# A message-passing network with experts on one core: the experts' input as a pipeline of tile groups

## What is computed

```python
h = jnp.maximum(_layernorm(x, axis=-1), 0.0)
x = x + _L3_gnn_ref(h, edge_index, ...)

def _L3_gnn_ref(x, edge_index, W_in, b_in, router_W, ...):
    h = x @ W_in + b_in                      # 3125 x 256
    for l in range(3):
        agg = segment_sum(h[src], dst) / deg
        logits = concatenate([h, agg]) @ router_W[l] + router_b[l]
        ...
        h = h + conf * moe
    return h @ W_out + b_out
```

## Time and profile before

| | |
|---|---|
| three runs, median | 3355.61 us |
| three runs, lowest and highest | 3353.94 and 3356.59 us |
| the profiled execution, its own time | 3354.32 us |
| its span, first to last instruction | 3352.3 us |
| mean granted clock of PE | 0.961 |
| busy: PE, DVE, ACT | 89%, 65%, 27% of the span |

### The profile page before, as it was taken

One profiled execution on the slowest core, in us unless ns is written; L12 is line 12 of the kernel. 1 busy time (PEld: TensorE's weight loads), 2 busy tenths in 40 slices (PEclk: granted clock), 3 DMA queues, 4 the chain that ended last, 5 costly groups with the idle time before them and its releaser, 6 DMA issues. The chain is left out here.

```text
span 3352.3 us, 47544 instructions
## 1 busy us (share of the span) xinstructions
PE 2990.9 (89%) x18761; PEld 1803.0 (54%) x18761; DVE 2184.1 (65%) x3982; ACT 897.6 (27%) x1667; POOL 16.6 (0%) x22
## 2 busy tenths in 40 slices
PE   3777889999797999999959999988999998999997
PEld 2555555555343444444535655664656564566565
DVE  7999555554426667666666666675666675666666
ACT  3887322121212000000023222323222233222222
POOL 1000000000000000000000000000000000000000
PEclk8898999999898999999979999998999998999999
DMA  4544456563003555554330000002000002000001
GB/s 103 155 140 145 134 184 205 189 209 125 21 1 116 172 154 171 171 155 130 88 104 4 6 3 4 3 3 80 3 4 4 5 1 82 3 4 3 4 3 40
DMA packets 310670, 262.56 MB, mean 78 GB/s; under 512 B 32735, under 2 KB 289377, under 8 KB 308142
## 3 DMA queue, kind: packets, MB, share of 16 engines
q1 hardware_dynamic: 295406, 252.86, 24.7%
q10 hardware_dynamic: 14624, 5.76, 0.7%
q0 software_dynamic: 416, 0.85, 0.1%
HBM read 171.03 MB, written 88.41 MB: 77 GB/s over the span
## 5 line engine op out<-in xcount | busy, mean ns | idle before, releaser
L1437 PE MATMUL psum<-r_wd,r_h 128*128 128x512 fp8e4 (+1 forms) x2600 | 567.9, 374 | 13.3 <-ACT r_h L226 12.7
L2057 PE MATMUL psum<-m_agg,m_weights 128*128 128x512 f16 (+2 forms) x2016 | 423.1, 362 | 34.2 <-ACT m_agg L1964 34.2
L2018 PE MATMUL psum<-counts,m_h 128*128 128x512 fp8e4 (+2 forms) x2100 | 416.0, 354 | 29.0 <-DVE m_h L1754 29.0
L2076 PE MATMUL psum<-m_weights,x_nodes 128*128 128x256 f16 (+1 forms) x3600 | 413.0, 273 | 17.6 <-DVE m_wtmp L1862 15.9
L1437 PEld LDWEIGHTS psum<-r_wd,r_h 128*128 128x128 f16 x2600 | 240.0, 96 | 306.1 <-issue 16.8
L2076 PEld LDWEIGHTS psum<-m_weights,x_nodes 128*128 128x128 f16 (+1 forms) x3600 | 350.3, 98 | 75.1 <-DVE m_wtmp L1862 22.6
L2057 PEld LDWEIGHTS psum<-m_agg,m_weights 128*128 128x128 f16 x2016 | 197.3, 101 | 243.1 <-issue 50.1
L2018 PEld LDWEIGHTS psum<-counts,m_h 128*128 128x128 f16 x2100 | 206.2, 98 | 225.3 <-issue 35.5
L1976 ACT ACTIVATE m_hT<-m_hT,m_g 128x256 f32<-128x256 f32 x300 | 135.4, 500 | 599.5 <-DVE m_hT L1876 599.5
L1964 ACT ACTIVATE m_agg<-psum,x_nodes 128x512 f32<-128x512 f32 (+2 forms) x336 | 236.4, 717 | 145.6 <-PE psum L2057 116.2
L627 PE MATMUL psum<-oh_c,oh_s 128*128 128x150 f16 x1566 | 159.4, 244 | 84.2 <-ACT counts L653 63.5
(11 more groups left out here) (284 smaller groups left out, 3363.6 us busy)
## 6 DMA issues: line engine op xcount, KB each, us to landing
r_wd<-packed_sym SPq DMA_DIRECT2D x120, 640.0 KB, 4.2
packed_counts<-strip SPq DMA_DIRECT2D x21, 1800.0 KB, 7.7
sym_blocks<-packed_counts SPq DMA_DIRECT2D x88, 384.0 KB, 4.5
packed_sym<-sym_blocks SPq DMA_DIRECT2D x84, 384.0 KB, 3.3
w_stage<-in_L_gnn_strong_W SPq DMA_DIRECT2D x12, 1024.0 KB, 6.4
m_weights<-in_L_gnn_strong_W SPq DMA_DIRECT2D x21, 512.0 KB, 9.3
w_stage<-in_L_gnn_weak_W SPq DMA_DIRECT2D x3, 1024.0 KB, 6.1
m_weights<-in_L_gnn_weak_W SPq DMA_DIRECT2D x12, 256.0 KB, 9.7
```

What stands on the lines that cost most here:

```text
L1437: m = pe.matmul(bank[pair[b]][:, 0:2 * cw], h16[:, part, p0 + i, :], f_[:, 2 * b:2 * b + 2, :], start=(p0 + i == 0 and part == 0), stop=(p ...
L2018: m = pe.matmul(bank[kb][:, 0:cw], h16[:, part, i, kb * P:(kb + 1) * P], A[:, i, c_:c_ + cw], start=(i == 0 and part == 0), stop=(i == NT ...
L2057: m = pe.matmul(bank[4 + hh % 2][:, 0:cw], w_[:, i, kb, f * P:(f + 1) * P], agg16[:, j, kb, 0:cw], start=(x_ == 0), stop=(x_ == len(todo) ...
L2076: m = pe.matmul(bank[b_][0:r_, 0:H], s_[:, pa[0] * BANK + k * P:pa[0] * BANK + k * P + r_], w_[:, pa[1], f, :], start=(f == 0 and pa == PA ...
```

## The change

The input stage becomes one pipeline by groups.

- ACT calls its copies from within the norm: ahead of step x come the copy of the turned group x-3 and, new, the copies of the products of group x-4 from PSUM into m_h, one for each tile.
- The bias goes into the product: ahead of each tile's product PE multiplies a block of ones on three partitions with three bf16 rows that add up to the f32 bias. DVE makes these rows in the relations stage (`bias_rows`, behind the counts of the first unit).
- DVE takes the largest absolute value of each group as it is finished (m_hmax), ahead of steps 6 to 9 of the norm and behind it. Layer 0 then reduces these seven values.
- The chain for the scales of the weights moves ahead of steps 0, 1 and 2 of the norm.
- The four DMAs move to the relations stage, behind ACT's part of its norm. The input weights and the bias rows lie in the room of m_bias, which is not used until layer 0, so the names of that tile stand in their rows.

Cut to the core:

```diff
@@ block_relations, ACT and DVE
                 norm.act()
+
+                act.dma_start(win, m_win).then_inc(win_in, 16)
+                act.dma_start(binw[:, 0, :], bass.AP(m_bin.tensor, m_bin.offset, [[0, 3], [1, H]])).then_inc(win_in, 16)
+                act.dma_start(wout[:], m_wout.rearrange("(k p) o -> p k o", p=P)).then_inc(wo_in, 16)
+                act.dma_start(bout[:], bass.AP(m_bout.tensor, m_bout.offset, [[0, P], [1, D]])).then_inc(wo_in, 16)
...
+                    for k in range(3):
+                        h_ = binh[:, k % 2, :]
+                        vec.tensor_copy(h_, left).then_inc(steps.handle, steps.up())
+                        settle()
+                        if k < 2:
+                            vec.tensor_tensor(left, left, h_, ALU.subtract).then_inc(steps.handle, steps.up())
...
+                    if (u, p0) == (1, PT):
+                        bias_rows()
@@ block_experts, ACT
-                    norm.act()
-                    for g, s in enumerate(GROUPS):
+                    def kept(g):
...
+                    def added(g):
+                        for i in range(GROUPS[g].start, GROUPS[g].stop):
+                            act.wait_ge(i_mixed, i + 1)
+                            act.activation(h2[:, i, :], bank[i % 6][:, 0:H], ACT.Copy).then_inc(i_added, 1)
+
+                    def behind(x_):
+                        if 0 <= x_ - 3 < NGR:
+                            kept(x_ - 3)
+                        if 0 <= x_ - 4 < NGR:
+                            added(x_ - 4)
+
+                    norm.act(among={x_: lambda x_=x_: behind(x_) for x_ in range(3, NGR + 2)})
+                    for x_ in range(NGR + 2, NGR + 4):
+                        behind(x_)
@@ block_experts, PE
-                        pe.wait_ge(i_kept, g + 1)
...
-                            pe.matmul(bank[i % 6][:, 0:H], xT[g % 2][:, k * P:(k + 1) * P], win[:], start=True, stop=True).then_inc(i_mixed, 1)
...
+                            pe.matmul(bank[i % 6][:, 0:H], ones3[:], bin3, start=True, stop=False)
+                            if k == 0:
+                                pe.wait_ge(i_kept, g + 1)
+                            pe.matmul(bank[i % 6][:, 0:H], xT[g % 2][:, k * P:(k + 1) * P], win, start=False, stop=True).then_inc(i_mixed, 1)
@@ block_experts, DVE
-                        vec.tensor_tensor(h2[:, i, :], bank[i % 6][:, 0:H], bin_[:], ALU.add).then_inc(i_added, 1)
...
+                    def largest(g):
+                        vec.wait_ge(i_added, GROUPS[g].stop)
+                        vec.tensor_reduce(hmax[:, g:g + 1], h2[:, GROUPS[g], :], axis=AX.XY, op=ALU.max, apply_absolute_value=True).then_inc(steps.handle, steps.up())
+
+                    first = {0: part_max, 1: part_spread, 2: part_kept}
+                    norm.dve(among={x_: first[x_] if x_ in first else (lambda x_=x_: largest(x_ - 6)) for x_ in range(NGR + 3) if x_ < 3 or x_ >= 6})
+                    for g in range(NGR - 3, NGR):
+                        largest(g)
@@ dve_layer
-                        vec.tensor_reduce(sc[:, 0:1], h2[:], axis=AX.XY, op=ALU.max, apply_absolute_value=True).then_inc(steps.handle, steps.up())
-                    else:
-                        vec.tensor_reduce(sc[:, 0:1], hmax[:], axis=AX.X, op=ALU.max).then_inc(steps.handle, steps.up())
+                    vec.tensor_reduce(sc[:, 0:1], hmax[:], axis=AX.X, op=ALU.max).then_inc(steps.handle, steps.up())
```

More of the change, by code:

```diff
@@ L1294, in maxima_pieces, with block_relations @@
                     yield l, t, i, rows_[:, c_:c_ + min(PIECE, rows_.shape[1] - c_)]
-    def block_relations(part):
+    def block_relations(part, win, bin3, wout, bout):
         PT = 5
@@ L1524, in behind, with bias_rows @@
                         vec.wait_ge(r_own_added, self_tiles_before(u) + nt)
+                def bias_rows():
+                    left, work = binw[:, 0, :], binw[:, 1, :]
+                    vec.wait_ge(win_in, 32)
+                    for k in range(3):
[5 more added lines that the diff above has]
+                        if k == 0:
+                            vec.tensor_scalar(work, h_, ident[0:3, k:k + 1], None, ALU.mult).then_inc(steps.handle, steps.up())
+                        else:
+                            vec.scalar_tensor_tensor(work, h_, ident[0:3, k:k + 1], work, ALU.mult, ALU.add).then_inc(steps.handle, steps.up())
+                        settle()
+                    vec.tensor_copy(bin3, work).then_inc(steps.handle, steps.up())
                 vec.memset(part[:], 0.0).then_inc(steps.handle, steps.up())
@@ L1547, in block_relations @@
             barrier()
-    prio_made, wo_in, parked, win_in, unparked, m_out = (sem(n) for n in ("prio_made", "wo_in", "parked", "win_in", "unparked", "m_out"))
+    prio_made, parked, unparked, m_out = (sem(n) for n in ("prio_made", "parked", "unparked", "m_out"))
     i_turned, i_kept, i_mixed, i_added, p_turned = (sem(n) for n in ("i_turned", "i_kept", "i_mixed", "i_added", "p_turned"))
@@ L1563, in build_program, with block_experts @@
     max_turned, max_spread = sem("max_turned"), sem("max_spread")
-    def block_experts(part):
+    def block_experts(part, win, bin3, wout, bout, bcast):
         SL = 2 * BANK
@@ L1617, in pe_inputs @@
                         pe.wait_ge(ln_scaled, norm.at(g))
+                        if g < 2:
+                            pe.wait_ge(steps.handle, mark[("part_spread", "part_kept")[g]])
                         if g >= 2:
@@ L2807, in network @@
             part = sbuf(c, "w_part", [P, 4, NLAY, 2], F32)
-            block_relations(part)
-            block_experts(part)
+            bcast = sbuf(c, "m_bias", [P, NE * H], F32)
+            win, bin3 = bcast[:, 0:H], bcast[0:3, H:H + H // 2].bitcast(BF16)
+            wout = sbuf(c, "m_wo", [P, KB, D], F32)
+            bout = sbuf(c, "m_bo", [P, D], F32)
+            block_relations(part, win, bin3, wout, bout)
+            block_experts(part, win, bin3, wout, bout, bcast)
     ok = nc.values_load(flag[0:1, 0:1], min_val=0, max_val=1)
```

57 lines of the change are left out of this document (27 added, 30 removed).

## The result

| | before | after |
|---|---|---|
| median (lowest to highest), 6 runs each | 3354.78 us (3346.57 to 3356.59) | 3369.19 us (3360.22 to 3377.13) |
| profiled execution, its own time | 3354.32 us | 3370.11 us |
| its span | 3352.3 us | 3365.1 us |
| mean granted clock of PE | 0.961 | 0.954 |
| input stage, first row of DVE to its last | 1683.65 to 1728.49: 44.84 us | 1684.81 to 1739.94: 55.13 us |

The ratio is 1.0045, with an interval from 1.0027 to 1.0063. 3348.0 us had been forecast, within 3344.5 to 3353.0: the time lies outside, on the other side of before.

A forecast was written before the change was run, and what follows sets the result against it. PE bounds the run; the input stage ran DVE's norm, then PE's products, end to end. Terms -8.0 + 0 + 0.4 = -7.6 us take 3354.32 to 3346.7; with 1.3 for the median, 3348.0 us, range 3344.5 to 3353.0.

The forecast's parts named there:

- Start of the stage: Input stage: first scaled group ready after 8.75 us where it was 8.19; PE turns group 0 at 1692.5.
- The clock: Input stage: PE's clock rises about the end of group 0, at 1698.6, after 5 us of work.
- The bias term: Input stage: each tile's bias product costs 0.15 us at full clock (0.12 to 0.20), 0.25 at the low one.
- C: Input stage: gaps during ACT's copies keep the clock at 1.2 GHz; 6.07 us a group, 3360.5 us; chance 9%.
- The pipeline itself: Input stage: groups 2 to 5 take 3.56 us each; stage term -8.0 us, between -9.0 and -5.2.
- Start of layer 0: Layer 0: the shorter reduce gains nothing, covered by ACT's DMA issue; bound -0.8 to +0.8 us.
- Relations stage: Relations stage: ACT's four load issues delay its copies, +0.4 us (0 to 2.8); bias rows on DVE cost nothing.
- A: Input stage: ACT's row of waits holds up DVE's norm; 4.3 us a group instead of 3.56, 3351.6 us; chance 15%.
- B: Layer 0: the shorter reduce pays too, another 6.66 us off, 3341.3 us; chance 6%.

The follow-up runs named there:

- e1: The changed kernel without the bias product, so b_in is left out of h; 3348.48 us, ratio 0.9971.
- e10: The changed kernel with the bias product on 64 rows instead of three; 3372.47 us in one run.
- e5: The changed kernel with the bias as one f32 row in place of three bf16 rows; 3386.33 us, ratio 1.0079.
- e9: The changed kernel without the pipeline: ACT's copies and DVE's largest values stand behind all of the norm again; 3380.35 us in one run.
- e2: The changed kernel with the bias product on 128 rows, 125 of them zero in the bias; 3349.82 us, ratio 0.9968.
- e3: The changed kernel with a group's four bias products together, ahead of its four f32 products; 3351.5 us, ratio 0.9988.
- e4: The changed kernel with 28 extra products on PE ahead of the first turn, without effect on the result; 3356.37 us, ratio 0.9995.
- e8: The changed kernel with the bias product on 128 rows and the experts' biases loaded by SP; 3326.83 us, ratio 0.9906.
- e7: The kernel before the change, with the loads of the experts' biases moved from ACT's queue to SP's; 3341.71 us, ratio 0.9951.
- e6: The changed kernel with the loads of the experts' biases moved from ACT's queue to SP's; 3349.1 us, ratio 0.9971.

## Why the prediction was wrong, step by step

**Start of the stage: right.** The first turn comes 8.61 us after the stage's first row (1693.42 - 1684.81); forecast 8.85.

**The clock: the step that failed most.** The prediction said of the end of group 0 "The clock rises about then, going by 5 us of work as before". It never rose. Five groups had been forecast in 18.1 us (3.9 and four of 3.56) and took 35.9 (five of 7.18). The row it went by is a row of one kind of work: turns and products of 128 rows. The busy time did not carry over to work of mixed rows: e1 is busy 4.91 of the 5.60 us ahead of its rise, while after is busy 5.63 of every 6 us and has no rise. In the runs, neighbours of unequal rows go with a clock that stays low (3, 64 or 1 row, with the pipeline or without: after, e10, e5, e9); with equal rows it rises (e1, e2), with few changes of rows too (e3), and once it is up the mixed work holds it (e4). That the bias product on fewer rows is the cause is shown by e2, which differs only in those rows and has 34.1 us. How it keeps the clock down stays open, for two readings fit all these runs: the change of rows as such, or theory W's first half, that the uncovered loads thin the work. A group of after spreads the four turns and four products that e1 does in 5.32 us over 7.18 us, and e5 over 10.05.

The trace of the kernel before shows that the second reading must be reckoned with. In layer 0 PE multiplies tiles by the router's weights (L2042), products of 9 columns on 128 rows, as are their neighbours. Its stretches, and its timeline:

```profile
1768.00:1770.00 2.00, 1.46 (x14) 1.00 0.33 115
...
1772.00:1774.00 2.00, 2.00 (x9) 0.50 0.00 0
```

```profile
1769.42 0.59 PE L2042 MATMUL psum<-m_rw,m_hT 128*128 128x9 f32 x4
...
1772.15 1.00 PE L2042 MATMUL psum<-m_rw,m_agg 128*128 128x9 f32 x4
```

PE has no idle time from 1768.54 on, no count of rows changes, and the clock falls to 0.50. In 8 of the 21 such stretches of that trace it falls, in or right behind them. So a low clock beside a full busy share needs no change of rows, and a busy share of the profile says little of the clock. A run with a thin product on 128 rows in the place of the bias would have separated the two readings; none was made.

**The bias term: the second.** The nearest rows had been taken for its bounds, 0.12 to 0.20 us at the full clock, 0.25 at the low one. The bound from above had 0.08 us for loads that don't hide; their lost cover costs 0.30 (0.84 in e4 less 0.54 in e2), with the bias product's own 0.11 together 0.41 at the full clock; at the low clock 0.61, since a tile without bias takes 0.86 (1.07 less the 0.21 of the bias in e2) and 1.475 with it. With 128 rows the term would have been right: 0.11 us, next to the 0.12 of the earlier trace rows. What I missed stands in the Trainium skill, TensorEngine Tiling (Array Packing), section Tiling Modes: a change of tiling mode drains TensorE, and its modes have 128, 64 or 32 rows. The trace agrees, if a plain product of 3 or 64 rows counts as a mode of its own, which no row shows: the loads that ran 0.42 us ahead with equal rows ran 0 us ahead with unequal ones, for 64 rows as for 3.

By these two steps the forecast of the stage, 36.85 us, becomes the 55.13 that were measured: group 0 +1.1 (7.18 for 6.07), the other five +17.8, start and tail -0.6. Of the 17.8 the clock alone, at C's 6.07 a group, would be 12.2, and the lost cover of the loads the other 5.6. (The prediction put a wholly slow group 1 at 2.0 us; by its own terms, 6.07 less 3.9, it is 2.2.)

**The pipeline itself: right, and worth more than forecast.** With the rows equal (e2, e8) a group takes 3.45 us (forecast 3.56) and the stage 34.1, 10.7 less than before, where the term was -8.0: the bias is shorter and the clock rises within group 0. ACT's copies of 256 columns come 0.30 us apart (four in 1.21; forecast 0.35). PE waited for nothing but ACT's turn copy.

**Start of layer 0: right.** The reduce paid nothing behind ACT's issue: the scale was there 9.0 us before ACT took it up. The measured +0.8 us is the bound given. e7 against e6 shows the other half, that it is worth 6.0 us and more without that issue.

**Relations stage: right, on the good side.** The four issues take 0.33 to 0.55 us each and end at 1067.25; ACT's first copy starts at 1068.10, with the same 2.40 us of idle time put down to PE as in the earlier trace rows. Cost 0, forecast 0.4. `bias_rows` takes 3.3 us of DVE (1097.07 to 1100.37) as estimated, and no engine waits for it. The last issue and the copy on ACT:

```profile
1066.76 0.49 ACTq L1463 DMA_DIRECT2D m_bo<-in_L_gnn_b_out  x1
1068.10 0.60 ACT L258 ACTIVATE r_ht<-psum 128x512 f32<-128x512 f32 x1 [2.40 <-PE psum L250]
```

**The rivals.** A, the lock step: DVE did wait for ACT's squares behind the copies (2.86 and 3.65 us at 1703.97 and 1711.15), but only because PE was slow; at the full clock e2 shows 3.45 us a group, under DVE's 4.3, so it didn't bind. B, the reduce pays too: it did not, for ACT's long issue was still there (7.13 us); e6 and e7 show that without it the reduce would have paid 6.0 us. C named the right outcome, a low clock throughout, by the wrong mechanism. It blamed the gaps while ACT copies; e1 has longer gaps of the same kind (0.69 to 0.78 us) and its clock rises, while e9 has those of after (0.36), e5 has none, and their clocks don't. Its price was low too, 6.07 us a group for 7.18, which made the stage 49.4 us long (to 1733.0 from 1683.65) and not 55.13. What weighed against C, that PE's share is larger now, came true (5.63 of 6 us) and the clock stayed low all the same.

## What to carry to other kernels

A product on fewer rows among products on 128 had two prices here that a sum over durations doesn't have: the weight loads around it lost their cover, and the clock did not rise. Try it with as many rows as its neighbours, zeros if need be; here that was the whole difference between 55 and 34 us. Don't take a high busy share as a sign that the clock will rise. Before paying for a result that comes earlier, look at what stands in the queue of the engine that takes it up: a DMA issue on a computing engine can be the longer wait, and moving it was worth more than the change it hid. And when whole runs spread more than the effect, compare profiles by stage.

## What was not expected of the hardware

- A granted clock of 0.50 for 45 us with PE busy 94% of the time (after), and for 40 us at 100% (e5), while e1 is busy 4.91 of 5.60 us ahead of its rise, and the 9-column products of the kernel before see the clock fall at 2.00 of 2.00 us.
- The same load (`bcast[:, 0:NWK * H]`) holds the issuing engine 7.13 us on ACT, behind five other issues; those five take 0.39 to 1.15 us there. Issued later, by SP, the same load takes 0.45 to 0.91 us in e6. What the long one waits for was not tried.
- Part of the spread between executions arises in a stretch that no kernel here changes. PE from 95 to 355 us, in before, after and e2:

```profile
95.00:355.00 260.00, 188.53 (x1978) 0.91 0.49 144
```

```profile
95.00:355.00 260.00, 187.97 (x1962) 0.91 0.48 143
```

```profile
95.00:355.00 260.00, 188.95 (x1851) 0.87 0.46 136
```

The counting stage at the start is granted 0.91 in before and in after, and 0.87 in e2, and the relations stage that follows begins at 1037.7, 1038.8 and 1050.8 us (the clearing of w_part). e2's profiled run was its slowest, 3361.43 us, with the input stage among the shortest. What decides the clock there was not tried.
